# One table set for logarithms and exponentials, two buffers of slot numbers, and the last shared group ahead of the key exponentials

## The reference

```python
x = x + tanh(g_xattn[0]) * attention(layernorm(x), ctx)          # 16 heads of 16, values rounded to 8 bits
x = x + tanh(g_ffn[0])   * moe0(layernorm(x))                     # 32 experts, 4 chosen per token, plus a shared expert of 704
x = x + tanh(g_xattn[1]) * wkv(layernorm(x), ctx)                 # a running sum over the 128 places of each sequence
x = x + tanh(g_ffn[1])   * moe1(layernorm(x))                     # 8 experts, 2 chosen, plus a shared expert of 352
# wkv, for each step with key k_t and value v_t:
y_t = (e1 * aa + exp(u + k_t) * v_t) / (e1 * bb + exp(u + k_t))   # aa, bb: sums of exp(k) * v and exp(k), fading by exp(-exp(decay))
# shared expert:
sh = silu(x @ sw_gate) * (x @ sw_up) @ sw_down
```

## Time and profile before

| what | value |
|---|---|
| time, median of 3 runs | 1297.46 us (1297.25 to 1297.59) |
| the profiled execution: its own time, its span | 1299.77 us, 1298.0 us |
| busy: PE, DVE, ACT, POOL | 1081.6 us, 969.6 us, 899.4 us, 696.8 us |
| chain that ended last, by engine | PE 42%, DVE 31%, ACT 10%, issue 7%, DMA 5%, POOL 4% |
| mean granted PE clock | 0.946 of full |

### The profile page before, as it was taken

One profiled execution on the slowest core, in us unless ns is written; L12 is line 12 of the kernel. 1 busy time (PEld: TensorE's weight loads), 2 busy tenths in 40 slices (PEclk: granted clock), 3 DMA queues, 4 the chain that ended last, 5 costly groups with the idle time before them and its releaser, 6 DMA issues.

```text
span 1298.0 us, 24037 instructions
## 1 busy us (share of the span) xinstructions
PE 1081.6 (83%) x8245; PEld 631.3 (49%) x8360; DVE 969.6 (75%) x1781; ACT 899.4 (69%) x1537; POOL 696.8 (54%) x610
## 2 busy tenths in 40 slices
PE   6958888888888888888888875998998697798992
PEld 4623444444444444444444653565544254456771
DVE  6999899999999999999999567233235687643334
ACT  4649899999999999999999653144406465533441
POOL 3016988887887888788787615276301000462331
PEclk9969999999999999999999977999999898699996
DMA  5686787888897888886676454199431021123335
GB/s 173 125 143 127 155 179 161 158 176 169 165 173 164 171 165 181 167 170 124 114 115 108 73 167 135 31 278 265 159 121 65 0 79 55 41 85 98 97 97 205
DMA packets 388191, 176.36 MB, mean 136 GB/s; under 512 B 329805, under 2 KB 373042, under 8 KB 388072
## 3 DMA queue, kind: packets, MB, share of 16 engines
q1 hardware_dynamic: 381368, 157.84, 55.7%
q0 software_dynamic: 6480, 16.77, 3.9%
q10 hardware_dynamic: 224, 0.20, 0.0%
HBM read 52.70 MB, written 43.59 MB: 74 GB/s over the span
## 4 chain that ended last, share of the span: by engine, by line
PE 42%; DVE 31%; ACT 10%; issue 7%; DMA 5%; POOL 4%; SPq 1%; POOLq 0%; DVEq 0%; ACTq 0%
DVE top L368 20%; PE bank L217 7%; PE bank L231 7%; ACT weight L411 6%; PE bank L2340 4%; PE bank L1081 3%; DMA answered_rows<-yrow,target 3%; PE bank L249 3%; PE bank L1064 3%; PE bank L2356 2%; PE bank L1068 2%; PE bank L1721 1%; PE bank L267 1%; DVE x_sb L2028 1%; POOL weight L463 1%
## 5 line engine op out<-in xcount | busy, mean ns | idle before, releaser
L411 ACT ACTIVATE weight<-bank,bias,sq_all 128x1024 uint8<-128x1024 f32 x512 | 610.0, 1200 | 32.4 <-PE bank L231 27.2
L368 DVE TENSOR_REDUCE top<-bank 128x1 f32<-128x512 f32 (+1 forms) x683 | 610.8, 951 | 16.1 <-PE bank L217 5.0
L463 POOL CAST weight<-turned 128x2048 bf16<-128x2048 uint8 x256 | 478.9, 1892 | 45.2 <-PE bank L249 24.7
L231 PE MATMUL bank<-kT,query 128*128 128x512 bf16 x915 | 285.7, 384 | 26.2 <-ACT weight L411 12.2
L249 PEld LDWEIGHTS bank<-v_sb,weight 128*128 128x128 bf16 x4096 | 172.1, 97 | 109.7 <-POOL weight L463 7.4
L217 PE MATMUL bank<-kT,qspace 64*128 64x512 bf16 x687 | 138.1, 395 | 63.2 <-DVE top L368 63.2
L249 PE MATMUL bank<-v_sb,weight 128*128 128x16 bf16 x4096 | 172.6, 170 | 6.3 <-POOL weight L463 5.9
L217 PE MATMUL bank<-kT,query 128*128 128x512 bf16 x331 | 127.0, 384 | 2.1 <-DVE top L368 1.4
L1697 POOL DMA_INDIRECT dispatched_rows<-qspace,put x32 | 33.9, 1060 | 152.6 <-DVE qspace L2130 144.0
L231 PEld LDWEIGHTS bank<-kT,query 128*128 128x128 bf16 x1024 | 60.1, 97 | 104.2 <-ACT weight L411 60.6
L411 ACT ACTIVATION_READ_ACCUMULATOR weight<-bank,bias,sq_all 128x1 f32 x512 | 101.5, 198 | 0.0
...
## 6 DMA issues: line engine op xcount, KB each, us to landing
...
```

The lines of the kernel that those rows point to most:

```text
L231: mm = pe.matmul(unit[u % 2][:, v * 512:(v + 1) * 512], query2[:, t % 2, h, :], kT[:, h // 2, first + v * 512:first + (v + 1) * 512], star ...
L368: ve.tensor_reduce(top[:, first:first + count], bank[:, first % 3:first % 3 + count, :], AX.X, ALU.max).then_inc(s_max, 1)
L411: ac.activation(weight8[:, n % BYTES, u * 1024:(u + 1) * 1024], unit[u], ACT.Exp, bias=bias[:, n:n + 1], scale=sq_all[:, n:n + 1], accum_o ...
L463: po.tensor_copy(weight[:, n % 3, :, :, :].rearrange("p c q two -> p (c q two)"), turned8[:, n % 3, :, :].rearrange("p c q -> p (c q)").bi ...
```

## The change

Three things are changed. First, a call preload_act_table_set names one set with both Ln and Exp at 12 places, so that the compiler puts no other load between a logarithm and an exponential; one of them is in the preparation, so that the attention's exponentials use this set too. The program has 29 loads in place of 52: in the front stage 5 in place of 9, in the mixing stage 20 in place of 40, in the preparation 4 in place of 3. Second, marked and numbered have two buffers each, so DVE and POOL wait for the product two groups before; POOL starts when the choices are marked, no longer when the destinations are written; and take_table stands two hidden chunks earlier on DVE. Third, in the mixing stage all chunks of the last shared group (group 3) come ahead of the exponentials of key groups 0 and 1, and DVE's calls are put in another order to go with it.

```diff
+            LOGS = "natural_log_exp_and_others"
@@ preparation, scalar
                     ac.activation(tgates[:], gates[:], ACT.Tanh).then_inc(s_prep_scalar, 1)
+                    ac.preload_act_table_set(LOGS)
@@ front_pool
-                    po.wait_ge(sm_["destinations_ready"], g + 1)
-                    if g > 0:
-                        po.wait_ge(sm_["table_products"], g)
+                    po.wait_ge(sm_["choices_marked"], g + 1)
+                    if g >= 2:
+                        po.wait_ge(sm_["table_products"], g - 1)
@@ front_vector, mark_slots
-                    else:
-                        ve.wait_ge(sm_["table_products"], g)
+                    if g >= 2:
+                        ve.wait_ge(sm_["table_products"], g - 1)
...
-                hidden0(0, 2, 5)
+                hidden0(0, 2, 3)
                 take_table()
-                hidden0(0, 5, 6)
+                hidden0(0, 3, 6)
@@ mixing_tensor
-                        answers0(2, 0)
-                        answers0(2, 1)
+                        for k in range(G):
+                            answers0(2, k)
+                        hidden0(3, 0)
                         turn_keys(0)
-                        answers0(2, 2)
+                        for c in range(1, NW0):
+                            hidden0(3, c)
+                        answers0(3, 0)
+                        answers0(3, 1)
                         keys_taken(0)
                         turn_keys(1)
-                        answers0(2, 3)
-                        for c in range(NW0 - 1):
-                            hidden0(3, c)
+                        answers0(3, 2)
+                        answers0(3, 3)
                         turn_mixed(0)
-                        hidden0(3, NW0 - 1)
-                        answers0(3, 0)
-                        answers0(3, 1)
                         mixed_taken(0)
                         turn_mixed(1)
-                        answers0(3, 2)
                         keys_taken(1)
                         turn_rows(0)
-                        answers0(3, 3)
@@ mixing_scalar
                         normalise(1, "first", "keys_normalised")
+                        shared_scalar(ac, 3, 0, NW0)
+                        ac.preload_act_table_set(LOGS)
                         exponentials(0)
                         exponentials(1)
-                        shared_scalar(ac, 3, 0, 1)
                         inverse(0)
-                        shared_scalar(ac, 3, 1, 3)
                         inverse(1)
-                        shared_scalar(ac, 3, 3, NW0)
...
                         silu1(1, 2)
+                        ac.preload_act_table_set(LOGS)
                         copy_rows(2)
@@ mixing_vector
                         answers0(2, 1)
-                        sum_keys(0)
                         answers0(2, 2)
                         answers0(2, 3)
+                        for c in range(NW0):
+                            hidden0(3, c)
+                        answers0(3, 0)
+                        sum_keys(0)
+                        answers0(3, 1)
                         denominators(0)
                         differences(0)
-                        hidden0(3, 0)
                         sum_keys(1)
-                        hidden0(3, 1)
-                        hidden0(3, 2)
+                        answers0(3, 2)
+                        answers0(3, 3)
                         denominators(1)
                         quotients(0)
                         differences(1)
-                        hidden0(3, 3)
-                        hidden0(3, 4)
+                        combine(2)
                         add_mixed(0)
-                        hidden0(3, 5)
                         quotients(1)
-                        answers0(3, 0)
-                        answers0(3, 1)
                         offsets(0, "second")
-                        combine(2)
-                        answers0(3, 2)
+                        offsets(2, "first")
                         add_mixed(1)
-                        offsets(2, "first")
-                        answers0(3, 3)
                         choose(0)
```

21 lines of the change are left out of this document (15 added, 6 removed).

## The result

The changed kernel takes **1306.18 us** (median of 4 runs, 1303.80 to 1308.66), the kernel before 1297.53 us in the runs beside it (4 runs, 1297.25 to 1300.09). The ratio is **1.0062, 95% interval 1.0040 to 1.0085**: slower by 0.6%. The forecast was 1298.7 with a range to 1303.5. The two profiled executions lie closer than the medians: 1303.80 (span 1302.0) against 1299.77 (span 1298.0), +4.0.

The account below looks back on a forecast made before the run. No engine was taken as full: the chain of waits through PE, DVE and ACT bounds it. Front -10.5 and mixing stage +11.7 give +1.2 us on the median 1297.5: 1298.7 us, range 1292 to 1303.5.

Parts of the forecast that it names:

- Front, -10.5: Front stage: three loads (3.85 us) and DVE's waits of 1.33 and 1.41 go; last product ends at 799.5, -10.5 us.
- the sign named for it: Front stage: if the table ends later than 802, DVE was not what bounds it.
- The table load: Front stage: each load costs 1.283 us, three 3.85; the Trainium skill's figure with drain would give 8.0.
- Attention, 0: Attention: its 512 exponentials from the joint set, and the preparation's new load, cost 0, with bounds of 2 us.
- Mixing steps 1 to 3, +18.4: Mixing stage, from PE's answers of group 2: the new order starts choose(0) at 1074.8, 18.4 us later.
- step 2: Mixing stage, DVE: all key work stands behind sum_keys(0) at 1025.7 and takes 39.7 us, to 1065.4.
- Step 4: PE after idling some 30 us: router(0) about 3.6, gate product twice 1.72; second block's first chunk 19.6 us late.
- what is given back: Later mixing stage: saved loads, shorter waits and PE's clock bring 19.6 us down to +11.7 at the last scatters.
- A: Rival: PE's clock is better than before, front -12.7, mixing +7.4, together -5.3: 1292.2 us; chance 0.26.
- B: Rival: half clock stays after the idling, mixing +14.9, 1301.9 us, if router(2) and answers exceed 8 us; chance 0.23.
- C: Rival: each table load holds ACT for its length again, 10.3 us more gained: 1288.4 us; chance 0.03.
- D: Rival: key work is not held back in the mixing stage, only saved loads count: 1281 us; chance 0.03.

Follow-up runs that it names:

- e8: e1 with the lane part of group 3's numbers done by ACT in place of POOL; ratio to the kernel before 0.9872.
- e1: The changed kernel with the mixing stage's old order on PE, DVE and ACT, joint table set and two buffers kept; 1282.31 us, ratio to before 0.9873.
- e3: The kernel before with the joint table set alone (14 preloads), orders and buffers as before; 1286.06 us, ratio 0.9912.
- e4: The kernel before with the two buffers, POOL's earlier start and the earlier take_table alone; 1293.40 us, ratio 0.9961.
- e6: e1 with the attention's exponentials from their own set again, the joint set loaded ahead of the front's first logarithm; ratio to before 0.9890.
- e15: The changed kernel with group 0's key work moved back between group 3's chunks on DVE and ACT, PE's order unchanged; ratio to before 1.0014.
- e10: The changed kernel run again unaltered, on another chip, with a second profiled execution; ratio to before 1.0050.
- e7: The changed kernel with offsets(2, "first") placed behind add_mixed(1) again; ratio to before 1.0066.
- e13: The changed kernel with 11 and 18 unread matrix products put into PE's two idle times in the mixing stage; ratio to before 1.0022.

## Why the prediction was wrong, step by step

The sum was -10.5 + 11.7 = +1.2. The profiled executions give -7.3 + 10.4 + 0.9 = +4.0; the medians +8.7.

- **Front, -10.5: 3.2 too much, the step of the mechanism that failed.** Of these 1.3 are POOL's, 0.9 lie between the attention's end and choose(1), 0.6 are the attention's later end, and 0.3 DVE's own work up to the last mark (27.80 us against 27.54). What failed is "the last group ... finishes 1 us ahead at worst", for POOL. I had the range of 4.0 to 6.0 us for a group of numbers and its start; in the trace it took 793.44 to 801.57, 8.1 us, since the lane part too met a mark. I let a mark stretch only the tile parts. e8 puts this at 1.3 us, and the sign named for it came: the table ended later than 802, at 802.65. From the attention's end to choose(1) the profiled execution won 3.0 us where 3.85 were forecast, but e1, with the same front, won 4.2: the difference is a wait for PE (3.34 us ahead of line 1366, 1.77 in e1), whose sixteen products before it took 5.50 us against 3.95. So the 0.9 is PE's and not the loads'. The attention itself ended 0.6 later. The rest, the waits of 1.33 and 1.41 that go, was right, and e3 and e4 show the two parts adding.
- **The table load.** Behind the last statistics and ahead of choose(1), no drain came back beside the 1.283 us per load: e3's last table product starts 62.3 us behind the attention's last statistics, 66.7 before. That is 4.4 us for three loads, and DVE's wait for PE ahead of line 1366 was also 1.0 us shorter there (1.94 against 2.98). By the figure of the Trainium skill (ScalarE: Activation LUTs, What ACT_TABLE_LOAD costs: load and drain, 2.66 us together) three would be 8.0. This case's traces side with the load alone.
- **Attention, 0: within its bounds of 2 us, but probably not 0.** The exponentials are as fast as before, yet the stage ended 1.1 us later on the mean of all traces (0.6 in the profiled execution); what that hangs on stays open (e6). e6 takes out the set and the preparation's new load together, so it can't tell which of the two, both put at 0, it was.
- **Mixing steps 1 to 3, +18.4: right in size** (18.1; the wait ahead of add_mixed(1) 5.37 against 5.8), but the reason given in step 2 was not the right one. That all key work stands behind 1025.7 is true (sum_keys(0) at 1018.69, 1026.0 on the old clock, and 39.6 us of DVE's work behind it, 39.7 forecast); but taking it away from there alone does not bring choose(0) forward. e15 took group 0's part away from there and gained 0.6. Moving combine(2) gained 5.9, moving turn_keys(1) 4.0, both 6.4: one hides part of the other, with the mixed rows' turns on PE behind them. The sum came out because DVE's queue was full in this order. What it lacked is a second chain of nearly the same length, over turn_keys(1) on PE and ACT's exponentials: in e15 sum_keys(1) still started 109.0 us behind S, against 108.3, and held choose(0) where it was.
- **Step 4 and what is given back: right in size, partly by other rows.** From choose(0) on 7.7 us came back where 6.7 were forecast (18.4 to 11.7). The gate product behind router(0) took 3.66 us, as forecast; it had taken 2.62 before, not 1.72. But router(0) was granted full clock (1.95, 3.6 forecast) in the profiled execution, and router(2) half (3.58) as before. In e10 router(0) ran at half clock, and S to choose(3) was 2.4 us longer.
- **Rivals.** A (a better clock everywhere, 1292.2) did not happen. B (half clock after the idle time, 1301.9) met its own condition, barely: router(2) and its answers took 3.58 + 4.57 = 8.15 us against 8. But its price, 3.2 us less given back, did not come in that execution (7.7 given back, 6.7 forecast). In e7, e10 and e13, where router(0) took 3.58 to 3.59, choose(0) to choose(3) is 83.6 to 84.3 us in place of 81.5, so 2.1 to 2.8 less was given back. C and D did not happen.
- **From the profile to the median: the largest part of the miss.** By the stages alone the time would have been 1301.5, inside the range. The remaining 4.7 us (8.7 by the medians, 4.0 by the profiled executions) are neither stage's. I set the difference of executions on a median, and took the 2.3 us by which before's profiled execution lay above its median as holding for the changed kernel, whose profile lay 2.4 us below its own. Before's profiled execution was slower than its median and the changed kernel's was the fastest of its four. Three runs of before within 0.3 us looked like a measure of the spread; 14 more of them, on another chip, ran from 1296.05 to 1302.30. Repeated on two more chips the changed kernel was at 1.0050 and 1.0055, 6.6 to 7.2 us (7.3 and 4.2 by the medians): part of the 8.7 was chance, and the range should have been about 3 us wider on each side for that alone.
